# Expert stage of a decoder layer on one Trainium2 core: the rows of two tiles turned together at every second tile

## The chip, the core and the metric

The kernel runs on one core of a Trainium2 chip. Its engines run side by side, each with its own program, and wait for each other by semaphores: TensorE (PE in the profile; its weight loads are PEld), VectorE (DVE), ScalarE (ACT), GpSimd (POOL) and SyncE (SP), which here only issues DMAs. PE writes to PSUM; the other data lies in SBUF or, behind DMAs, in HBM. The metric is the device time of one execution in microseconds, as a median over runs.

## The reference

A decoder layer over 32 sequences of 256 tokens, 256 channels, in float32. Three blocks follow each other, each with a residual and a layer norm: a Mamba-2 mixer, cross attention to 77 context rows with 16 heads, and a mixture of experts. Only the last is touched by the change:

```python
scores = xt @ gate_w                                   # 8192 tokens, 8 experts
ew, ei = jax.lax.top_k(scores, K)                      # K = 2
ew = jax.nn.softmax(ew, axis=-1)
mask = ei[None, :, :] == jnp.arange(E)[:, None, None]
wE = jnp.sum(ew[None, :, :] * mask, axis=-1)
h = jax.nn.gelu(jnp.einsum('td,edf->etf', xt, w1) + b1[:, None, :], approximate=False)
o = jnp.einsum('etf,efd->etd', h, w2) + b2[:, None, :]
y = _layernorm(xt[None, :, :] + o, ln_g[:, None, :], ln_b[:, None, :])
out = jnp.einsum('et,etd->td', wE, y)
```

## The kernel before, in words

The stages are the mixer, keys and values, attention (which also sends every token's row to two places in HBM, sorted by expert), the experts, and a last stage that joins each token's two shares and normalises.

The expert stage (`experts_phase`) works on 71 tiles (2 x 8192 / 256 + 7) of 256 rows, each of one expert; a table in SBUF tells each tile's first row and expert. For tile t:

- SP loads the expert's first weights, `load_w1` (L1034, 1024 KB, high and low halves, into one of 4 places; and the bias, L1036), and then the tile's 256 rows, `load_rows` (L1041, 260 KB, into one of 8 buffers `xa`). It does so three tiles ahead: in step t it issues the weights of tile t + 3 and behind them the rows of tile t + 3. The weights' place is free once up and gelu of tile t - 1 are done, so SP waits for these (`s_h`, `s_gelu` of `t.ago(head.W)`). The first three tiles are loaded at the end of the attention stage.
- PE turns the rows, `turn_x` (L2010): four 128x128 transposes into one of two PSUM buffers `ps_x`. It waits for the tile's rows (`s_xa_in`) and for the low half of tile t - 2, which was read from the same PSUM buffer (`s_xlo`).
- ACT copies the turned rows as the high half `xT_hi` (`x_high`, L2054), DVE forms the low half `xT_lo` (`x_low`, L2090). Both wait until up of tile t - 2 is done, since that reads the same two-deep buffers.
- PE forms the hidden values, `up` (L112 to L114, into `ps_h`): 24 matmuls of 128x128 by 128x256, three for each product (high by high, high by low, low by high).
- ACT applies gelu (L2068) and takes the high half (`h_high`, L2077); DVE takes the low half (`h_low`, L2102).
- PE forms the output, `down` (L112 to L114, into `ps_o`), again 24 matmuls. The second weights of all experts stay in SBUF.
- DVE adds, takes the norm's statistics and scales; POOL adds the bias row, forms the inverse deviation, and sends the result back by an indirect DMA (L2197).

Each engine's order is written out by `run_steps`: a list of parts with lags, run for every tile; the first 8 tiles and the last ones are written out, the rest is a loop whose turn holds 8 tiles (`per=X`). `t.slot` is the tile's number modulo 8, `t.ago(-1)` the next tile. PE's list is: turn of the next tile, up of this tile, down of the tile before. Before the list starts, `turn_x` of tile 0 is run. The list is fixed; no planner or pool decides anything.

Of the kernel before, what the change touches and what calls it, by code (L numbers as in the profile page):

```python
# [77 lines left out]
def run_steps(eng, n, stages, spare=0, per=2, peel=PEEL):  # L78

    last = max(lag for _, lag in stages)
    turns = (n - spare - peel) // per
    after = peel + turns * per

    def peeled(s):
        for stage, lag in stages:
            if 0 <= s - lag < n:
                stage(Item(*divmod(s - lag, per), per))

    for s in range(peel):  # L90
        peeled(s)
    with eng.Fori(peel // per, peel // per + turns) as turn:
        for slot in range(per):
            for stage, lag in stages:
                stage(Item(turn, slot, per).ago(lag))
    for s in range(after, n + last):
        peeled(s)
# [10 lines left out]
def split3(eng, out, lhs, rhs, start, stop):  # L108

    (lh, ll), (rh, rl) = lhs, rhs
    eng.matmul(out, lh, rh, start=start, stop=False)  # L112
    eng.matmul(out, lh, rl, start=False, stop=False)  # L113
    return eng.matmul(out, ll, rh, start=False, stop=stop)  # L114
# [894 lines left out]
class ExpertsHead:  # L1009

    X = 8
# [900 lines left out]
def experts_phase(nc, signals, done_with, routing, b1, weights, w2, head):  # L1913
# [4 lines left out]
    n_tiles = routing.n_tiles  # L1918
    X = head.X

    with ExitStack() as ctx:
        def sb(name, shape, dt=F32):
            return ctx.enter_context(nc.sbuf_tensor("c_" + name, shape, dt))
# [7 lines left out]
        spare = sb("spare", [P, 1])  # L1931
# [40 lines left out]
        def expert_of(eng, t):  # L1972
            return eng.value_load(routing.table[0:1, 1, bass.ds(t.value(), 1)], min_val=0, max_val=E - 1)

        @block.sync
        def _(sp):
            def load_rows(t):
                if not t.before(X):
                    sp.wait_ge(s_xb, t.ago(X).count(1, 1))
                    sp.wait_ge(s_to, t.ago(X).count(1, 1))  # L1980
                    sp.wait_ge(s_share, t.ago(X).count(1, 1))
                    sp.wait_ge(s_x, t.ago(X).count(1, 1))
                    sp.wait_ge(s_os, t.ago(X).count(1, 1))
                head.load_rows(sp, routing, t)

            def load_w1(t):
                if not t.before(head.W):
                    sp.wait_ge(s_h, t.ago(head.W).count(1, 1))
                    sp.wait_ge(s_gelu, t.ago(head.W).count(1, 1))
                head.load_w1(sp, routing, b1, t)  # L1990

            def rows_ahead(t):
                if not (t.known() and t.value() + 3 >= n_tiles):
                    load_rows(t.ago(-3))

            def w1_ahead(t):
                if not (t.known() and t.value() + 3 >= n_tiles):
                    load_w1(t.ago(-3))

            run_steps(sp, n_tiles, [(w1_ahead, 0), (rows_ahead, 0)], spare=3, per=X, peel=8)  # L2000

        @block.tensor
        def _(pe):
            def turn_x(t):
                pe.wait_ge(s_xa_in[t.slot], t.turn * 16 + 16)
                if not t.before(2):
                    pe.wait_ge(s_xlo, t.ago(2).count(1, 1))
                for k in range(KD):
                    for c in range(NT):
                        last = pe.transpose(ps_x[t.par][:, T * k + P * c:T * k + P * c + P],  # L2010
                                            xa[t.slot][:, c, P * k:P * k + P], ident)
                last.then_inc(s_x, 1)

            def turn_x_next(t):
                if not (t.known() and t.value() + 1 >= n_tiles):
                    turn_x(t.ago(-1))

            def up(t):
                pe.wait_ge(s_w1_in[head.place(t)], head.loaded(t))
                pe.wait_ge(s_xhi, t.count(1, 1))  # L2020
                pe.wait_ge(s_xlo, t.count(1, 1))
                if not t.before(2):
                    pe.wait_ge(s_gelu, t.ago(2).count(1, 1))
                for m in range(MF):
                    for k in range(KD):
                        part, at = 2 * k + m // 2, slice(P * (m % 2), P * (m % 2) + P)
                        last = split3(pe, ps_h[t.par][:, m // 2, T * (m % 2):T * (m % 2) + T],
                                      (w1[head.place(t)][:, part, 0, at], w1[head.place(t)][:, part, 1, at]),
                                      (xT_hi[:, t.par, k, :], xT_lo[:, t.par, k, :]), k == 0, k == KD - 1)
                last.then_inc(s_h, 1)  # L2030

            def down(t):
                e = expert_of(pe, t)
                pe.wait_ge(s_hlo, t.count(1, 1))
                if not t.before(2):
                    pe.wait_ge(s_y, t.ago(2).count(NT, NT))
                for c in range(NT):
                    for m in range(MF):
                        at = slice(T * m + P * c, T * m + P * c + P)
                        last = split3(pe, ps_o[t.par][:, D * c:D * c + D], (h_hi[:, t.par, at], h_lo[:, t.par, at]),  # L2040
                                      [w2[:, bass.ds(MF * e + m, 1), h, :].rearrange("p o d -> p (o d)")
                                       for h in range(2)], m == 0, m == MF - 1)
                last.then_inc(s_o, 1)

            turn_x(Item(0, 0, X))
            run_steps(pe, n_tiles, [(turn_x_next, 0), (up, 0), (down, 1)], spare=3, per=X, peel=8)

        @block.scalar
        def _(act):
# [400 lines left out]
```

## Time and profile before

| | |
|---|---|
| median of 3 runs | 2335.59 us (2334.3 to 2337.23) |
| the profiled execution | 2338.11 us, its span 2336.3 us |
| PE busy over the span | 2146.5 us, 92% |
| DVE, ACT, POOL busy | 73%, 62%, 49% |
| mean granted clock of PE | 0.943 |
| the expert stage | about 1779 to 2229 us of the span |

Times in the profile count from the span's start. Shares over the whole span mix stages that have different limits, so the expert stage has to be looked at by itself.
### The profile page before, as it was taken

Reading aid. Unit: us, or ns where it says so; the run is one execution under the profiler, and the core shown is the slowest. Engines: PE = TensorE matmul, PEld = TensorE weight load, DVE = VectorE, ACT = ScalarE, POOL = GpSimd, SP = SyncE. Lnnn points to the kernel's source line nnn. Section 1 sums busy time; section 2 is a strip of 40 time slices with the busy share of each in tenths; the row PEclk is TensorE's granted clock in tenths of the full one; section 3 lists DMA queues with packets and bytes.
Section 4 is the critical chain, followed back from the end, with each engine's and each line's share of the span. In section 5 each row is a group of like instructions: output and inputs, shape, how many; then the busy total and the mean of one; then the engine's idle time right before and its main releaser. Section 6 shows DMA issues by size and latency. Waiting matters only on the chain. (4 is left out here: it accounts for less than half of the span.)

```text
span 2336.3 us, 53128 instructions
## 1 busy us (share of the span) xinstructions
PE 2146.5 (92%) x15740; PEld 1915.1 (82%) x15741; DVE 1717.0 (73%) x4450; ACT 1444.1 (62%) x3032; POOL 1153.9 (49%) x1376
## 2 busy tenths in 40 slices
PE   6989999898997797999999999999995999999968
PEld 5878888787886786888888888888885999999934
DVE  5877778787776324677776777767764999999956
ACT  6777777777775333666666666666662555555525
POOL 2556565555655001234343443334332777777767
PEclk8999999999998898999999999999997999999955
DMA  4443443434342353232222222222215878787658
GB/s 131 149 159 131 142 147 130 159 113 159 127 146 100 138 206 118 68 97 77 72 76 71 82 67 74 74 81 73 67 47 178 262 253 260 255 262 254 197 165 290
DMA packets 200152, 330.44 MB, mean 141 GB/s; under 512 B 26300, under 2 KB 87492, under 8 KB 200068
## 3 DMA queue, kind: packets, MB, share of 16 engines
q1 hardware_dynamic: 187108, 293.75, 38.5%
q0 software_dynamic: 12960, 35.67, 4.1%
q8 instruction: 41, 0.67, 0.1%
q14 instruction: 43, 0.35, 0.0%
HBM read 176.20 MB, written 153.15 MB: 141 GB/s over the span
## 5 line engine op out<-in xcount | busy, mean ns | idle before, releaser
L1605 ACT ACTIVATE b_wk_f<-b_ps_s,b_nmx 128x77 f32<-128x77 f32 x1024 | 233.7, 347 | 17.5 <-DVE b_nmx L1651 17.5
L619 DVE SCALAR_TENSOR_TENSOR a_conv<-a_xc_pad,a_cw,a_conv 128x256 f32<-128x256 f32 x384 | 218.7, 630 | 2.6 <-ACT a_conv L493 2.6
L1613 ACT ACTIVATE b_pT<-b_ps_pT 77x1024 f32<-77x1024 f32 x128 | 130.7, 1021 | 141.2 <-PE b_ps_pT L1511 141.2
L2068 ACT ACTIVATE c_hid<-c_ps_h,c_b_c 128x256 f32<-128x256 f32 x284 | 111.3, 475 | 159.8 <-PE c_ps_h L114 157.7
L2197 POOL DMA_INDIRECT made_scratch<-c_o_s,c_to x142 | 164.1, 1155 | 87.4 <-issue 49.9
L1876 POOL DMA_INDIRECT sent_scratch<-b_x_t,b_pos x128 | 128.4, 1003 | 141.8 <-DVE b_x_t L1747 102.0
L1667 DVE TENSOR_TENSOR k_wk_lo<-b_ps_oT,k_wk_lo 128x512 fp32r<-128x512 f32 x128 | 88.0, 688 | 128.3 <-ACT k_wk_lo L1619 100.6
L1596 ACT ACTIVATE b_qT<-b_ps_q,b_bq_s 128x256 f32<-128x256 f32 x256 | 107.5, 471 | 105.9 <-PE b_ps_q L114 104.7
L1892 POOL CAST w<-k_c_f 128x256 f32 (+1 forms) x32 | 14.7, 460 | 318.0 <-DMA k_c_f<-in_c_w 318.0
L112 PE MATMUL c_ps_o<-w,c_h_hi 128*128 x568 | 162.2, 286 | 6.9 <-DVE c_h_lo L2102 6.8
L114 PE MATMUL c_ps_o<-w,c_h_lo 128*128 x568 | 161.1, 284 | 0.0
L1499 PE MATMUL b_ps_s<-b_kz,b_qT 128*128 128x154 f32 x1024 | 156.3, 294 | 5.2 <-ACT b_wk_f L1605 5.1
L113 PE MATMUL c_ps_o<-w,c_h_hi 128*128 x568 | 161.0, 284 | 0.0
L112 PE MATMUL b_ps_out<-b_wo_hi,k_wk_lo 128*128 128x256 f32 x512 | 158.3, 309 | 0.0
L112 PE MATMUL b_ps_q<-k_wk_hi,b_wq_hi 128*128 128x256 f32 x512 | 154.3, 301 | 2.4 <-DVE k_wk_hi L1643 1.5
L1499 PEld LDWEIGHTS b_ps_s<-b_kz,b_qT 128*128 128x128 f32 x1024 | 140.4, 189 | 6.0 <-issue 6.0
L113 PE MATMUL b_ps_out<-b_wo_lo,k_wk_lo 128*128 128x256 f32 x512 | 144.5, 282 | 0.0
L114 PE MATMUL b_ps_q<-k_wk_hi,b_wq_lo 128*128 128x256 f32 x512 | 143.6, 281 | 0.0
L113 PE MATMUL b_ps_q<-k_wk_hi,b_wq_hi 128*128 128x256 f32 x512 | 143.6, 280 | 0.0
L114 PE MATMUL b_ps_out<-b_wo_hi,k_wk_lo 128*128 128x256 f32 x512 | 143.5, 280 | 0.0
L1524 PE MATMUL b_ps_oT<-b_pT,b_vv 77*64 77x256 f32 x1024 | 138.8, 392 | 0.0
L112 PEld LDWEIGHTS b_ps_out<-b_wo_hi,k_wk_lo 128*128 128x128 f32 x512 | 96.3, 188 | 48.9 <-issue 48.9
(314 smaller groups left out, 7776.6 us busy)
## 6 DMA issues: line engine op xcount, KB each, us to landing
sent_scratch<-r_none SPq DMA_DIRECT2D x90, 780.0 KB, 6.0
b_wq_hi<-parts_scratch SPq DMA_DIRECT2D x18, 1024.0 KB
b_wq_lo<-parts_scratch SPq DMA_DIRECT2D x18, 1024.0 KB
k_wk_hi<-parts_scratch SPq DMA_DIRECT2D x18, 1024.0 KB
k_wk_lo<-parts_scratch SPq DMA_DIRECT2D x17, 1024.0 KB
d_got<-made_scratch SPq DMA_DIRECT2D x32, 512.0 KB, 5.0
keys_scratch<-k_k_s SPq DMA_DIRECT2D x8, 1232.0 KB, 4.7
b_kz<-keys_scratch SPq DMA_DIRECT2D x64, 154.0 KB, 2.8
```

The lines of the kernel that those rows point to most:

```text
L112: eng.matmul(out, lh, rh, start=start, stop=False)
L113: eng.matmul(out, lh, rl, start=False, stop=False)
L114: return eng.matmul(out, ll, rh, start=False, stop=stop)
L619: dve.scalar_tensor_tensor(out=conv[:, m, :], in0=xc_pad[:, m, k:k + L], scalar=cw[:, m, k:k + 1], in1=conv[:, m, :], op0=ALU.mult, op1=AL ...
L1499: last = pe.matmul(s_scores[:, i, 2 * j:2 * j + 2, :], qT[:, u.par, i, P * j:P * j + P], kz[:, b.par, :, GM * g + i, :], start=True, stop= ...
L1524: last = pe.matmul(ps_oT[HD * a:HD * a + HD, L * i:L * i + L], vv[:, b.par, at:at + HD], pT[:, u.par, i, L * a:L * a + L], start=True, sto ...
L1596: last = act.activation(qT[:, u.par, i, :], ps_q[:, L * i:L * i + L], ACT.Identity, bias=bq_s[:, m:m + 1], scale=HD ** -0.5)
L1605: last = act.activation(pe_[:, u.par, c, :], s_scores[:, c // (C // GM), c % (C // GM), :], ACT.Exp, bias=nmx[:, u.par, c:c + 1])
L1613: act.activation(pT[:, u.par, :, :], ps_pT[0:LK, :, :], ACT.Copy).then_inc(s_pTc, 1)
L1876: pool.indirect_dma_start(routing.sent, bass.IndirectOffsetOnAxis(pos[:, b.par, 2 * c + n:2 * c + n + 1], 0), x2_t[:, b.par, c, :], None). ...
L2068: last = act.activation(hid[:, t.par, T * m:T * m + T], ps_h[t.par][:, m // 2, T * (m % 2):T * (m % 2) + T], ACT.Gelu, bias=b1_c[:, head.p ...
L2197: pool.indirect_dma_start(routing.made, bass.IndirectOffsetOnAxis(to[:, t.slot, c:c + 1], 0), o_s[:, t.par, c, :], None).then_inc(s_sent[t ...
```

## The change

PE's list gets another first part. It does nothing at odd tiles. At an even tile t it turns the rows of tile t + 1 and of tile t + 2, one behind the other. Up, down, all other engines' lists and all buffers are as before.

```diff
-            def turn_x_next(t):
-                if not (t.known() and t.value() + 1 >= n_tiles):
-                    turn_x(t.ago(-1))
+            def turn_next_two(t):
+                if t.slot % 2 == 0:
+                    for more in (1, 2):
+                        if not (t.known() and t.value() + more >= n_tiles):
+                            turn_x(t.ago(-more))
...
             turn_x(Item(0, 0, X))
-            run_steps(pe, n_tiles, [(turn_x_next, 0), (up, 0), (down, 1)], spare=3, per=X, peel=8)
+            run_steps(pe, n_tiles, [(turn_next_two, 0), (up, 0), (down, 1)], spare=3, per=X, peel=8)
```

The order of PE's instructions at the start of the stage, before. In brackets stand the semaphores that an instruction waits for, under the names of their first users: `a_na` is `s_xlo` here, `a_l` is `s_xhi`, `a_sp` is `s_gelu`; `c_xa_in1` tells of the rows in buffer 1, `c_w1_in0` of the weights in place 0. The tiles `b_wk_f`, `b_w_stage` and `k_c_f` hold the row buffers, `b_mk` the identity, `b_wq_*` and `k_wk_*` the weights.

```order
L2010 MATMUL c_ps_x<-b_mk,b_wk_f 128x128 [waits c_xa_in0]
L2010 MATMUL c_ps_x<-b_mk,b_wk_f 128x128 x3
L2010 MATMUL c_ps_x<-b_mk,b_wk_f 128x128 [waits c_xa_in1]
...
L112 MATMUL c_ps_h<-c_xT_hi,b_wq_hi 128x256 [waits a_na,a_l,c_w1_in0]
L113 MATMUL c_ps_h<-c_xT_lo,b_wq_hi 128x256
```

And after the change, at the same place on PE:

```order
L2010 MATMUL c_ps_x<-b_mk,b_wk_f 128x128 [waits c_xa_in0]
L2010 MATMUL c_ps_x<-b_mk,b_wk_f 128x128 x3
L2010 MATMUL c_ps_x<-b_mk,b_wk_f 128x128 [waits c_xa_in1]
...
L2010 MATMUL c_ps_x<-b_mk,b_wk_f 128x128 [waits a_na,c_xa_in2]
...
L112 MATMUL c_ps_h<-c_xT_hi,b_wq_hi 128x256 [waits a_na,a_l,c_w1_in0]
L113 MATMUL c_ps_h<-c_xT_lo,b_wq_hi 128x256
```

The turn of tile 2 now stands ahead of the first up, and so does its wait for the rows in buffer 2 (its three further transposes, and those of tile 1, are left out, since they read alike). The second place is the even tile 2 and the odd tile 3 on PE, as a piece of the difference:

```order
 L2010 MATMUL c_ps_x<-b_mk,b_w_stage 128x128 [waits a_na,c_xa_in3]
 L2010 MATMUL c_ps_x<-b_mk,b_w_stage 128x128 x3
+L2010 MATMUL c_ps_x<-b_mk,b_w_stage 128x128 [waits a_na,c_xa_in4]
+L2010 MATMUL c_ps_x<-b_mk,b_w_stage 128x128 x3
 L112 MATMUL c_ps_h<-c_xT_hi,k_wk_hi 128x256 [waits a_na,a_sp,a_l,c_w1_in2]
 L113 MATMUL c_ps_h<-c_xT_lo,k_wk_hi 128x256
...
 L114 MATMUL c_ps_o<-w,c_h_lo 128x256
-L2010 MATMUL c_ps_x<-b_mk,b_w_stage 128x128 [waits a_na,c_xa_in4]
-L2010 MATMUL c_ps_x<-b_mk,b_w_stage 128x128 x3
 L112 MATMUL c_ps_h<-c_xT_hi,k_wk_lo 128x256 [waits a_na,a_sp,a_l,c_w1_in3]
 L113 MATMUL c_ps_h<-c_xT_lo,k_wk_lo 128x256
```

The turn of tile 4, with its wait for the rows in buffer 4 and for `s_xlo` of tile 2, moved from in front of up(3) to in front of up(2). The same holds for every even tile up to 70.

## Rows read from the trace of the kernel before

**Rows 1.** The page: GB/s moved, in 40 slices of the span.
```profile
GB/s 131 149 159 131 142 147 130 159 113 159 127 146 100 138 206 118 68 97 77 72 76 71 82 67 74 74 81 73 67 47 178 262 253 260 255 262 254 197 165 290
```

**Rows 2.** Windows: busy us of PE, PEld, DVE, ACT, POOL; clock, DMA share, GB/s.
```profile
1900.00:2000.00 100.00, 100.00 (x854) 100.00 (x853) 97.18 (x298) 53.81 (x101) 78.43 (x82) 1.00 0.79 260
```

**Rows 3.** Timeline of PE: start us, us, engine, line, operation, out<-in, shapes.
```profile
1993.94 0.60 PE L2010 MATMUL c_ps_x<-b_mk,b_w_stage 128*128 128x128 f32 x4
1994.29 0.37 PE L112 MATMUL c_ps_h<-c_xT_hi,k_wk_hi 128*128 128x256 f32 x1
1994.50 0.28 PE L113 MATMUL c_ps_h<-c_xT_lo,k_wk_hi 128*128 128x256 f32 x1
1994.61 0.28 PE L114 MATMUL c_ps_h<-c_xT_hi,k_wk_hi 128*128 128x256 f32 x1
...
1997.11 0.28 PE L112 MATMUL c_ps_o<-w,c_h_hi 128*128 x1
...
2006.33 0.36 PE L112 MATMUL c_ps_h<-c_xT_hi,b_wq_hi 128*128 128x256 f32 x1
...
2012.13 0.60 PE L2010 MATMUL c_ps_x<-b_mk,k_c_f 128*128 128x128 f32 x4
```

**Rows 4.** Timeline of DVE, same step.
```profile
1995.20 1.21 DVE L2102 TENSOR_TENSOR c_h_lo<-c_hid,c_h_hi 128x1024 fp32r<-128x1024 f32 x1
```

**Rows 5.** Waits from 1820 to 2240: who <- whom: us in total, times, longest.
```profile
PE c_ps_o L112 <- DVE c_h_lo L2102: 4.6, 4, 2.8
```

**Rows 6.** Timeline of ACT, same step; in brackets the idle time before.
```profile
1997.36 1.57 ACT L2068 ACTIVATE c_hid<-c_ps_h,c_b_c 128x256 f32<-128x256 f32 x4 [2.19 <-PE c_ps_h L114]
```

**Rows 7.** DMAs that SyncE issues, timeline.
```profile
1776.74 0.37 SPq L1041 DMA_DIRECT2D b_wk_f<-sent_scratch  x1
...
1999.93 0.37 SPq L1034 DMA_DIRECT2D k_wk_hi<-parts_scratch  x1
...
2001.90 0.37 SPq L1041 DMA_DIRECT2D k_c_f<-sent_scratch  x1
```

**Rows 8.** Windows at the load of tile 38.
```profile
2000.00:2000.50 0.50, 0.50 (x6) 0.50 (x5) 0.50 (x3) 0.02 (x1) 0.42 (x1) 1.00 0.00 0
2005.50:2006.00 0.50, 0.50 (x7) 0.50 (x6) 0.50 (x2) 0.50 (x1) 0.45 (x1) 1.00 0.57 223
2006.00:2006.50 0.50, 0.50 (x7) 0.50 (x6) 0.50 (x2) 0.04 (x1) 0.44 (x1) 1.00 0.04 16
```

**Rows 9.** Timeline of DVE at the start of the stage.
```profile
1781.23 0.69 DVE L2090 TENSOR_TENSOR c_xT_lo<-c_ps_x,c_xT_hi 128x512 fp32r<-128x512 f32 x1 [1.67 <-ACT c_xT_hi L2054]
```

**Rows 10.** Timeline of PE at the start of the stage.
```profile
1779.48 1.94 PE L2010 MATMUL c_ps_x<-b_mk,b_wk_f 128*128 128x128 f32 x8 [17.41 <-PEq L1281]
1782.07 0.55 PE L112 MATMUL c_ps_h<-c_xT_hi,b_wq_hi 128*128 128x256 f32 x1 [0.65 <-ACT c_xT_hi L2054]
...
1792.85 0.38 PE L112 MATMUL c_ps_o<-w,c_h_hi 128*128 x1 [2.17 <-DVE c_h_lo L2102]
```

**Rows 11.** Windows beside up(4), up(32), up(50) and up(68).
```profile
1809.72:1810.22 0.50, 0.50 (x7) 0.50 (x6) 0.50 (x6) 0.22 (x1) 0.42 (x2) 1.00 0.05 12
...
1981.52:1982.02 0.50, 0.50 (x7) 0.50 (x6) 0.50 (x2) 0.20 (x1) 0.50 (x1) 1.00 1.08 404
...
2091.47:2091.97 0.50, 0.50 (x7) 0.50 (x6) 0.50 (x2) 0.21 (x1) 0.38 (x2) 1.00 0.67 261
...
2202.95:2203.45 0.50, 0.50 (x7) 0.50 (x6) 0.47 (x2) 0.00 (x0) 0.50 (x1) 1.00 0.40 139
```

**Rows 12.** Windows at the start of the stage.
```profile
1770.50:1781.00 10.50, 1.52 (x7) 1.55 (x8) 0.06 (x1) 0.40 (x1) 0.00 (x0) 0.50 0.80 251
1782.00:1786.00 4.00, 3.93 (x18) 3.96 (x19) 0.69 (x1) 0.06 (x1) 0.00 (x0) 0.50 1.05 390
1794.00:1797.00 3.00, 3.00 (x16) 3.00 (x15) 1.23 (x1) 0.46 (x1) 0.00 (x0) 0.50 1.07 386
```

**Rows 13.** DMA issues: out<-in, count, KB each, median us to landing.
```profile
b_xa<-x_scratch SPq DMA_DIRECT2D x32, 256.0 KB, 2.7
```

## Prediction

> **What bounds the kernel now.** I read the page first, then the busy sums by stretch, then each engine's timeline within one step of the expert stage, and last the share of the DMA engines in windows of half a microsecond. The page's slices show the DMA rate tripled in the last quarter: that is the expert stage [rows 1]. Between 1900 and 2000 us the tensor engine (PE) is busy 100% at a granted clock of 1.00, VectorE (DVE) 97%, ScalarE (ACT) 54%, GpSimd (POOL) 78%, the DMA engines 79% [rows 2]. So PE sets the pace there and DVE is close behind. What makes PE wait in this stage goes into the time; what only frees another engine doesn't.
>
> T(k) is the turn of tile k (four transposes), up(k) and down(k) its two products. PE's timeline has T(35) at 1993.94, up(34) from 1994.29, down(33) from 1997.11, and T(38) at 2012.13: three steps in 18.19 us, 6.06 each, with no gap [rows 3]. DVE's low half of the hidden values of tile 33 is ready at 1996.41 (1995.20 + 1.21), 0.70 before down(33) starts [rows 3, 4]. From 1820 to 2240 PE waits 4 times for DVE, 4.6 us together, 2.8 of them in one; the rest, 1.8, is what DVE costs PE [rows 5].
>
> **The change, part by part.** The numbers of transposes, matmuls, loads and activations stay. T(odd) stays at its place, ahead of up of the even tile before it. T(even) moves forward over one up and one down, and over the waits that these have.
>
> (a) Entries. From the turn's first transpose to the second matmul of up it is 0.56 us (1993.94 to 1994.50), five starts at 0.112; a plain matmul comes 0.11 after its predecessor (1994.50, 1994.61) [rows 3]. The mixture costs at most 0.01 us per entry, 34 entries fewer give 0.4. Bounds: 0; and, if the first matmul's 0.37 us against 0.28 [rows 3] were lost time, 34 x 0.09 = 3.1. I take 0.4, since starts tell the pace and ends are modelled.
>
> (b) Shift inside a pair. Up(even) and down(odd) come one turn later, 0.35 us (1993.94 to 1994.29 [rows 3]); the next up and down stand at their old time. ACT waits 2.19 us for up [rows 6], so it starts the gelu of even tiles 0.35 later and still meets the 0.70 of DVE's lead, which itself grows by 0.35 for odd tiles. Nothing.
>
> (c) The new wait. Here I expect the time to go. T(k) needs the 256 rows of tile k. Take k = 38. SyncE issues its loads when gelu(34) is done: the weights at 1999.93, the rows behind them at 2001.90 [rows 7]. The DMA share is 0.00 in 2000.0 to 2000.5, still 0.57 in 2005.5 to 2006.0, and 0.04 after that [rows 8]. The rows are last in the queue, so they are there at about 2005.9. T(38) is at 2012.13 today, 6.2 us later. In the changed program it stands right behind T(37), at 2006.33, where up(36) begins today [rows 3]. Up(34), and with it gelu(34) and the load, is 0.35 later by (b), so the rows come at about 2006.25; from a release to PE's first matmul it takes 0.15 more (x_low ends at 1781.92, up(0) starts at 1782.07 [rows 9, 10]). 2006.4 against 2006.33: a lead of a whole step has become nothing. When T(k) waits, up(k-2), down(k-3) and all of PE's queue stand behind it; later loads hang on later gelus, so they move too and the loss is not made up.
>
> How often, and how much? For each even k from 6 to 70 (33 tiles) I took the half microsecond before the start of up(k-2) and the one after it. The earlier window begins where, in today's clock, the rows would have to be there (start - 0.35 - 0.15). In 9 of the 33 the second window still has a share of 0.05 or more: late by 0.5 to 1.0, I take 0.75, sum 6.75. In 19 only the first has: late by 0 to 0.5, I take 0.25, sum 4.75. In 5 neither has. [Rows 11] are the second window of tile 6 (first tile), the first windows of 34 and 52, and the first of 70 (last tile). A share of 0.06 is one of 16 DMA engines, and one is enough to hold a load up. Sum 11.5. Bounds: some of the nine (6, 18, 54, 66) show more in the second window than in the first and may be other transfers; with the other 5 at 0.5 alone it is 2.5; with 9 at 1.0 and 19 at 0.5 it is 18.5.
>
> The Trainium skill ("DMA: Bandwidth & Descriptors", section "Why a DMA increments its semaphore by 16 and not by 1") says that only the full 16 increments mean that all data is there, because the engines finish independently. It speaks against this change. The small shares at the end of the loads agree with it; by a rule that a load is as good as landed when most engines are done, the sum above would be near its lower bound, 2.5.
>
> (d) Start of the stage. Today T(0) and T(1) start at 1779.48, up(0) at 1782.07, and T(2) is done before PE's idle 2.17 us that end with down(0) at 1792.85 [rows 10]; there it costs nothing. Changed, T(2) stands ahead of up(0) and needs rows issued at 1776.74 [rows 7]. Asked for until then: two tiles' weights and three tiles' rows, 2 x 1.05 + 3 x 0.27 = 2.9 MB. Moved: 10.5 us x 251 KB = 2.64 MB up to 1781.0, the rest at 390 KB per us: done at 1781.7; with the next weights, which share the engines, at 1784.4 [rows 12]. I take 1783.0. On the half clock (0.50, 18 matmuls in 3.93 us [rows 12]) four transposes take 0.87, so up(0) starts at about 1784.0, 1.9 late. If the clock rises when it does today, the matmuls put off run at full speed and 1.1 is left; if it rises as long after up(0), 1.9. I take 1.4. Bounds: 0.5 (rows there at once) and 4.7 (rows at 1784.4, and 1.5 more on half clock after a longer idle).
>
> (e) What goes. With PE slower, DVE catches up, and PE's 1.8 us for DVE mostly go: -1.5 (bounds 0 and -1.8).
>
> Sum: -0.4 + 11.5 + 1.4 - 1.5 = +11.0 us. The profiled execution took 2338.11, its span 2336.3; it becomes 2349.1. The median of the runs shown, 2335.59, lies 2.5 below it; with the same difference the median becomes 2346.6. What a measurement of this kernel can't tell from no change is 0.2%, 4.7 us.
>
> **Rivals.**
> No change: the loads land in time. DMAs, less crowded by the wider gap before even tiles, end a few tenths earlier. For it: many of the 19 first windows have a share of only 0.07 to 0.2. Against it: 1.08 and 0.67 at tiles 34 and 52 [rows 11]. Term (c) at its lower bound: -0.4 + 2.5 + 1.4 - 1.5 = +2.0, 2337.6. Chance 0.16.
>
> Faster: entries cost what the durations say. -3.1 - 1.8 = -4.9, with all loads in time and a start that costs nothing: 2330.7. It wins only if (c) is below about 3 us. Chance 0.05.
>
> Slower still, by the clock. After the idle 2.17 us before 1792.85 the clock stands at 0.50 in 1794 to 1797, where 16 matmuls take 3.0 us [rows 10, 12]; at the 0.115 of [rows 3] they would take 1.8. If waits of a microsecond or two bring this about five times, 6 us, and (c) is 18.5: -0.4 + 18.5 + 1.4 - 1.5 + 6 = +24.0, 2359.6. For it: an idle PE is what preceded that fall. Against it: most of the waits are under half a microsecond. Chance 0.13.
>
> Slower by the landing. A load of 256 KB in another stage takes 2.7 us to landing [rows 13], of which 0.7 is moving at 390 KB per us and 0.6 or more goes before the first byte (1999.93 to after 2000.5); up to 1.4 may pass between the last byte and the semaphore. If the windows leave that out, each of the 33 tiles is 1.4 later, 46 us: 2393. Against it: the shares count the engines until they report. Chance 0.03. The skill's page has the same thing in "Anatomy of one DMA — SWDGE (gpsimd) path", as a fixed part of some 2 us, most of it waiting for the write's receipt; no row here separates it.
>
> **Numbers.** Forecast 0.61, its own range 2341 to 2354; the rivals 0.16, 0.05, 0.13, 0.03; that the order of instructions isn't as shown, 0.02, no change. Slower by over 0.2% (above 2340.3) is 0.61 + 0.13 + 0.03 + 0.01 = 0.78; within 0.17; faster 0.05. The range of all, 2337 to 2357, takes in the rival of no change and most of the way to the clock's.
>
> **What would show it.** Right: waits of PE (or its weight loads) in the turn, ended by the load of rows, at 20 to 28 even tiles, most under 1 us, the longest at few tiles; a pair of steps of 12.1 us growing to about 12.4; DVE busy near 95%; fewer waits of PE for DVE; up(0) at about 1784. Wrong: PE without gaps from 1900 to 2000 and a span within 3 us: then the rows land earlier than the shares say. Wrong in the other direction: a granted clock below 1.00 inside the stage.

## The result and the profile after

| | before | after |
|---|---|---|
| median, us | 2334.95 (2333.21 to 2337.23) | 2359.3 (2353.13 to 2369.24) |
| the profiled execution, us | 2338.11 | 2360.27 |
| its span; mean granted clock | 2336.3; 0.943 | 2358.5; 0.945 |
| up(0), up(70) start at | 1782.07, 2215.37 | 1779.75, 2236.89 |

The ratio is 1.0107, with a 95% interval of 1.0087 to 1.0126: slower by 24.4 us, where 11 had been forecast, and outside the range. Here and below, medians of the kernels with an edit leave out slow executions, those over 1.5% above the fastest of the same kernel; for the kernel before this would make 0.03 us of difference at most.

Of the 22.2 us between the spans 21.5 are there when up(70) starts. They are made up of three parts. From up(3) to up(70) it is 411.7 us before and 436.3 after, 24.6 more. From T(0) to up(3) it is 24.2 and 25.5, 1.3 more. And T(0) itself, with which the stage begins on PE, came 4.4 us sooner in the changed kernel's execution (1775.07, against 1779.48 in [rows 10]), which can't come from the change, since T(0) stands ahead of it on PE; other executions of the kernels below have T(0) anywhere from 1767 to 1780. So the loss is made in the expert stage, nearly all of it behind its start. Lines of the code are two higher after the change (L2102 is now L2104); L2010 is unchanged.

The page after, its row of GB/s in 40 slices, answers to [rows 1]: 262, 253, 260, 255 have become 245, 236, 242, 240. The stage moves the same bytes in more time.

```profile
GB/s 139 141 156 158 117 158 129 141 157 117 158 117 104 152 216 101 72 83 74 83 69 73 72 80 72 71 75 75 71 42 238 245 236 242 240 241 242 197 163 289
```

Windows of the changed kernel (us; busy of PE, PEld, DVE, ACT, POOL; clock; DMA share; GB/s), the first against [rows 2]:

```profile
1900.00:2000.00 100.00, 94.42 (x793) 92.83 (x792) 94.70 (x271) 47.49 (x90) 69.52 (x76) 1.00 0.73 236
...
1793.20:2247.00 453.80, 429.96 (x3599) 422.21 (x3598) 431.49 (x1242) 218.16 (x413) 315.02 (x341) 1.00 0.72 231
```

PE is no longer busy all the time, 94.4 us of 100 with 793 matmuls instead of 854. Every other engine is less busy too. VectorE, at 94.7, stands level with PE, but it was at 97.2 before; what bounds the stage has to be read from what PE waits for. The granted clock is 1.00 from 1793.2 to 2247. Who PE waits for is in the waits from 1795 to 2260 (who <- whom: us in total, times, longest), against [rows 5]:

```profile
PEld c_ps_x L2010 <- issue: 23.5, 26, 1.7
PE c_ps_x L2010 <- DMA b_wk_f<-sent_scratch: 8.8, 12, 1.4
PE c_ps_x L2010 <- DMA k_c_f<-sent_scratch: 6.1, 7, 1.5
...
PE c_ps_o L112 <- DVE c_h_lo L2104: 5.0, 4, 2.8
PE c_ps_x L2010 <- DMA b_w_stage<-sent_scratch: 3.7, 6, 1.0
```

The new waits are the three on `sent_scratch`, the rows, in the turn: 25 times. (The 23.5 us of PEld stand before the same turns: its weight loads stand still with PE.) Measured from start to start of PE's instructions (0.12 apart where nothing waits), it is 30 places of the 34 pairs, 23.3 us, median 0.72, longest 1.63; before there is none. Each of them lies between the two turns of a pair. Late downs, counted in the same way at the first two matmuls of each down, are 3.4 us at 12 places before and 2.1 at 5 after.

### The profile page after: what moved, and what is told of

Its sections match the earlier page's. It is cut to its first block and busy times, and to the rows that moved or that the text cites. A ratio compares the mean times of both kernels' runs of the same rounds, so it can differ in the third digit from the quotient of the medians.

```text
span 2358.5 us, 53121 instructions
## 1 busy us (share of the span) xinstructions
PE 2148.0 (91%) x15740; PEld 1909.4 (81%) x15741; DVE 1731.0 (73%) x4450; ACT 1440.1 (61%) x3032; POOL 1147.4 (49%) x1376
```

## One circle, and why it has a length

The timeline of the changed kernel from up(32) to up(34) (start us, us, engine, line, operation, out<-in, and idle time before with what ended it). SPq rows are SyncE's issues.

```profile
1991.14 0.65 PE L2010 MATMUL c_ps_x<-b_mk,b_wk_f 128*128 128x128 f32 x4 [1.15 <-DMA b_wk_f<-sent_scratch]
1991.55 0.36 PE L112 MATMUL c_ps_h<-c_xT_hi,b_wq_hi 128*128 128x256 f32 x1
...
1993.80 0.96 POOL L2199 DMA_INDIRECT made_scratch<-c_o_s,c_to  x1 [0.30 <-issue]
...
1994.36 0.28 PE L114 MATMUL c_ps_h<-c_xT_hi,b_wq_hi 128*128 128x256 f32 x1
...
1995.48 1.57 ACT L2070 ACTIVATE c_hid<-c_ps_h,c_b_c 128x256 f32<-128x256 f32 x4 [4.77 <-PE c_ps_h L114]
...
1997.93 0.37 SPq L1034 DMA_DIRECT2D b_wq_hi<-parts_scratch  x1
...
2000.08 0.19 SPq L1041 DMA_DIRECT2D b_w_stage<-sent_scratch  x1
...
2004.64 0.65 PE L2010 MATMUL c_ps_x<-b_mk,b_w_stage 128*128 128x128 f32 x4 [1.01 <-DMA b_w_stage<-sent_scratch]
2005.04 0.36 PE L112 MATMUL c_ps_h<-c_xT_hi,k_wk_hi 128*128 128x256 f32 x1
```

Read it as a circle: T(34) waited for its rows, so up(32) is at 1991.55; gelu(32) ends at 1997.05 and lets SyncE issue the weights of tile 36 at 1997.93 and its rows at 2000.08; they are all there at 2004.52; T(36) starts 0.12 us later, and up(34) at 2005.04. That is 13.49 us for a pair of steps, in which PE has work for 12.25. The pieces, as means over the even tiles 8 to 66 of each trace, all in us (up to gelu's end; to the weights' issue; to the rows' issue; to their landing; to the next even up):

| profile | pieces | pair | late increments | late rows issues |
|---|---|---|---|---|
| before | 4.79, 0.97, 1.98, 4.36, (no wait) | 12.29 | 6 | 2 |
| changed, first time | 5.00, 0.90, 2.19, 4.45, 0.57 | 13.10 | 23 | 6 |
| changed, fourth time | 4.74, 0.90, 1.95, 4.55, 0.55 | 12.69 | 0 | 0 |

The fourth time is the run of the last comparison below. The first line shows what could have been worked out ahead of the change: its four pieces add up to 12.10 us, and with the 0.57 from the landing to the next even up the circle would be 12.67. That is 0.38 over the pair of 12.29, times 33 pairs 12.5 us, an estimate.

Two things are counted at the right. A late increment is one of the semaphore behind up (`s_h`): by the trace's semaphore events it comes 0.29 us after the start of up's last matmul, but at 23 of 71 tiles of the first trace 0.47 to 1.08 us after, at nearly all of them 1.3 to 1.6 us behind the start of one of POOL's indirect sends. Above, the last matmul starts at 1994.36 and gelu 1.12 us later; at most tiles it is 0.37. A late rows issue is one where SyncE needs 3.0 us and not 1.95 from the weights to the rows, as here for tile 40, with POOL's two sends beside it (timeline of the changed kernel):

```profile
2024.32 0.37 SPq L1034 DMA_DIRECT2D b_wq_hi<-parts_scratch  x1
2024.49 1.04 POOL L2199 DMA_INDIRECT made_scratch<-c_o_s,c_to  x1 [0.71 <-issue]
...
2025.83 0.96 POOL L2199 DMA_INDIRECT made_scratch<-c_o_s,c_to  x1 [0.30 <-issue]
...
2027.26 0.01 SPq L1041 DMA_DIRECT2D b_wk_f<-sent_scratch  x1
```

## Experiments

Each diff is against the changed kernel, where nothing else is said. "Before" is the kernel before, run in the same comparison.

**Is it the wait for rows?** SyncE issues the rows ahead of the weights, some 5 us sooner; once with pairs, once in the kernel before.

```diff
-            run_steps(sp, n_tiles, [(w1_ahead, 0), (rows_ahead, 0)], spare=3, per=X, peel=8)
+            run_steps(sp, n_tiles, [(rows_ahead, 0), (w1_ahead, 0)], spare=3, per=X, peel=8)
```

> The changed kernel, but SyncE issues in each step the rows of tile t+3 before the weights of tile t+3, so the rows no longer stand behind the wait for gelu of tile t-1 nor behind a megabyte of weights. Theory A (the time goes into T(even) waiting for its rows): the waits of PE in L2010 for a load disappear, PE has no gaps in the stage, and the time is that of the kernel before, 2333 to 2338 us. Rival B (two turns in a row, or up and down of a pair shifted by a turn, cost by themselves, by the hidden values coming later to ACT and DVE): the time stays above 2350 us. Rival C (half of each): about 2345.

> The kernel before with the same swap of SyncE's two loads: the control for the experiment above. The rows are early anyway, so theory A says no change: 2335 us within 0.2%. If the order of loads were worth something by itself (weights later, fewer collisions), it would show here and would have to be taken off the run above; a loss would show as PE waiting for the weights in up.

Pairs: 2340.36 against 2333.18, ratio 1.0032 [1.0008, 1.0056]. Single turns: 2333.01, 1.0006 [0.9986, 1.0026]. No wait was left in the turn, so the rows were the cause of those. But with pairs another loss stood in their place: late downs of 17.7 us at 31 places (1.7 with single turns). After the longest of them, an idle PE for 2.06 us before a down at 2119.71, the granted clock was 0.50 from 2120.5 to 2123.5, where 16 matmuls took 3.0 us. Waits from 1795 to 2260, that window, and one of VectorE's smallest operations beside POOL's bias addition:

```profile
PE c_ps_o L112 <- DVE c_h_lo L2104: 16.6, 13, 2.7
```

```profile
2120.50:2123.50 3.00, 3.00 (x16) 3.00 (x16) 2.92 (x10) 0.00 (x0) 2.22 (x3) 0.50 0.63 198
```

```profile
2099.79 1.84 DVE L2143 TENSOR_SCALAR c_ve<-c_mv 128x2 f32<-128x2 f32 x1
2100.28 1.31 POOL L2176 TENSOR_TENSOR c_xb<-b_wk_f,b_w_stage 128x512 f32<-128x512 f32 x1
2102.81 1.21 DVE L2104 TENSOR_TENSOR c_h_lo<-c_hid,c_h_hi 128x1024 fp32r<-128x1024 f32 x1
2104.30 0.38 PE L112 MATMUL c_ps_o<-w,c_h_hi 128*128 x1 [1.52 <-DVE c_h_lo L2104]
```

VectorE's 128x2 operation ends with POOL's addition (2101.63 and 2101.59), 1.84 us where it takes 0.17 alone; 11 of 71 took over 1.5 us here, 3 before. The Trainium skill ("SBUF — State Buffer", section "SBUF: two separate sides") says that the two engines share a pair of ports, and that whichever of their operations starts first holds it for its whole instruction while the other stands. That the two end together agrees with one being held by the other. That the one recorded as starting first (2099.79 against 2100.28) is the one held does not agree, as far as POOL's recorded start is exact, and the measurement decides. Of VectorE the section names only operations in a two-port mode or with two inputs in SBUF; whether this one is of that kind no row shows.

**The size of the circle.** The rows go between the weights and the bias, instead of behind both.

```diff
-        sp.dma_start(self.b1_c[:, self.place(t), :], b1[bass.ds(e, 1), :, :].rearrange("o p m -> (o p) m")
-                     ).then_inc(self.s_w1_in[self.place(t)], 16)
+        return lambda: sp.dma_start(self.b1_c[:, self.place(t), :], b1[bass.ds(e, 1), :, :].rearrange("o p m -> (o p) m")
+                                    ).then_inc(self.s_w1_in[self.place(t)], 16)
...
+                    load_bias = load_w1(t.ago(-3))
+                    load_rows(t.ago(-3))
+                    load_bias()
```

> The changed kernel, but SyncE issues the 2 KB of bias behind the rows and not between weights and rows. The rows are issued about 0.56 us earlier; everything else stays. Theory A with a cycle that closes over two steps (turn, up, gelu, load, turn of the next even tile): every even tile that waits gets about 0.5 us less, so 34 x 0.5 = 17 us of the 24 go, and the time is 2340 to 2348. Theory A without the cycle (each wait a separate accident of a late DMA, as I forecast): those accidents stay and it is above 2350. Rival B (pairs cost by themselves): no difference, 2355 to 2362.

2340.33, ratio 1.0034 [1.0021, 1.0047]. The rows' issue came 1.38 us behind the weights and not 1.95, but from there to their landing it took 4.96 instead of 4.55 (the changed kernel's fourth profile, taken on another chip, but like this one without late increments). Of 0.56 us 0.41 were lost again; that the weights ahead in the queue still have to move would explain it, but is not shown by itself. What is left made the pair 12.50 instead of 12.69, times 33 is 6 us; the waits are 6.8 us at 27 turns, median 0.18, instead of 11.7, and the time 7 us less against before (+7.2, +14.1). The time follows the circle; the expected 17 us took the landing as fixed.

**The same pairs with a longer lead.** The second turn stands behind up instead of ahead of it.

```diff
-            run_steps(pe, n_tiles, [(turn_next_two, 0), (up, 0), (down, 1)], spare=3, per=X, peel=8)
+            run_steps(pe, n_tiles, [(turn_more(1), 0), (up, 0), (turn_more(2), 0), (down, 1)], spare=3, per=X, peel=8)
```

`turn_more(n)` turns tile t + n at even t.

> The changed kernel with T(t+2) of the even tile moved behind up(t), ahead of down(t-1): 3 us later than in the change, 3 us earlier than in the kernel before. Up and down of a pair shift as little as before. Theory A: a lead of some 3 us over the landing is enough, no wait, 2333 to 2338 us. Rival D (an early turn costs by itself because its PSUM buffer, ACT's x_high or DVE's x_low come in another order): half of the loss or more stays, above 2345.

2330.62, ratio 0.9991 [0.996, 1.0021]; no wait in the turns, late downs 3.6 us, up(3) to up(70) 410.9. Three microseconds later, the rows are always there, in a comparison whose profiles had no late increments.

**The start of the stage, and the rest without it.** Once only the turn of tile 2 moves; once the pairs begin at tile 2.

```diff
-                if t.slot % 2 == 0:
-                    for more in (1, 2):
-                        if not (t.known() and t.value() + more >= n_tiles):
-                            turn_x(t.ago(-more))
+                first = t.known() and t.value() == 0
+                if not (t.known() and t.value() in (1, n_tiles - 1)):
+                    for more in (1, 2) if first else (1,):
+                        turn_x(t.ago(-more))
```

```diff
-                if t.slot % 2 == 0:
-                    for more in (1, 2):
+                single = t.known() and t.value() < 2
+                if single or t.slot % 2 == 0:
+                    for more in (1,) if single else (1, 2):
```

> Only the turn of tile 2 moves ahead of up(0); from there on each turn stands one tile ahead, as before the change. Theory of the cycle (all of the loss is made anew at each even tile, the start costs nothing): 2333 to 2335 us, ratio 1.000 to 1.001, up(3) to up(70) 411 to 413 us. Rival, the prediction's term for the start: +1.4 us, and by its upper bound +4.7. A rival beyond both: a late start puts all engines of the stage into another phase, in which the loads stay late; then up(3) to up(70) is well above 413 here as well.

> The complement: the first turns stand as before the change, pairs begin at the even tile 2. Theory of the cycle: the whole loss, 2356 to 2360 us, ratio about 1.010, 28 to 33 waits in the second turn of a pair with 21 to 25 us. Rival, the start carries part of it: 2350 or less.

Start alone: 2334.32 against 2333.12, 1.0004 [0.9985, 1.0024]. Pairs from tile 2 on: 2345.51, 1.0054 [1.0025, 1.0083], with 11.2 us of waits at 25 turns. The two parts add up to 13.6 us, where the whole change had lost 24.4. This profile had no late increment.

**VectorE and POOL.** POOL adds the bias row behind the inverse deviation, with pairs and rows first, and in the kernel before.

```diff
-            run_steps(pool, n_tiles, [(add_b2, 1), (scale, 2), (send_back, 3)], spare=3, per=X, peel=8)
+            run_steps(pool, n_tiles, [(scale, 2), (add_b2, 1), (send_back, 3)], spare=3, per=X, peel=8)
```

> Pairs, with the rows issued ahead of the weights, and besides POOL adds the bias row after the inverse deviation and no longer before it. In the kernel with rows first alone there were no waits for rows, but 19 us of waits of PE for VectorE's low half; in the stretches with these waits VectorE's smallest operation (c_ve, 128x2) took up to 1.8 us beside POOL's bias addition, instead of 0.17. Theory D (this collision is what makes VectorE late): c_ve goes to 0.2 to 0.5 us everywhere, PE's waits for VectorE drop under 5 us, time 2333 to 2336. Rival E (VectorE is late because gelu of even tiles starts 0.35 us later behind the pair, and only its lead counts): waits of 10 us or more remain although c_ve is short, 2340 us or more. Rival F: the addition collides with VectorE's other operations at its new place, and VectorE's whole step gets longer.

> The kernel before the change with POOL's bias addition behind the inverse deviation, as a control for the run with pairs. Theory D: within 0.2% of before, perhaps 1 to 3 us faster, since PE's 3.4 us of late downs go. Rival F: slower by 3 us or more, by a longer step of VectorE.

2398.19 and 2396.25, ratios 1.0278 [1.0251, 1.0305] and 1.0274 [1.0246, 1.0302]. Rival F has the sign, and theory D is left undecided, because the edit changed more than the collision. The short operation did fall, from a mean of 588 ns in the kernel before to 203, but VectorE now waits for POOL's sends (28.7 us in 200 over its three groups of `c_o_s`). DVE groups of the second kernel from 1900 to 2100 (busy, mean ns, idle before and what ended it):

```profile
L2156 DVE SCALAR_TENSOR_TENSOR c_o_s<-c_tt,c_rw,b_wk_f 128x256 f32<-128x256 f32 x24 | 12.2, 550 | 11.6 <-DMA made_scratch<-c_o_s,c_to 11.5
...
L2141 DVE TENSOR_SCALAR c_ve<-c_mv 128x2 f32<-128x2 f32 x28 | 5.7, 203 | 1.0
```

**Is the changed kernel's 24 us repeatable?** The two kernels again, the rows-first one again, and both cures together.

> The changed kernel itself once more, beside the kernel before, on another day or chip than the first comparison. In its first profile an even tile's circle (rows there, up, gelu, weights issued, rows issued, rows there) measured 5.00 + 0.90 + 2.19 + 4.45 + 0.57 = 13.1 us, in the run with pairs from tile 2 on 4.73 + 0.90 + 1.94 + 4.55 + 0.54 = 12.65. The first difference, 0.27, are increments of the semaphore behind up that came 0.5 to 0.8 us late at 20 of 71 tiles, the second, 0.25, rows issues of SyncE that came 3.0 instead of 1.95 us behind the weights at 6 even tiles. Theory G: both are a disturbance of that run and not of the program; the changed kernel then measures 2344 to 2349 here, ratio 1.005 to 1.007, and the profile shows pairs of steps of about 12.65 us. Rival H: the early turn of tile 2 at the start is what puts the stage into that phase; then this run gives 2353 to 2362 again, ratio about 1.010, with late increments at 15 tiles or more.

> The kernel before the change itself, for its profile. In its first profile 5 tiles had a late increment behind up (0.54 to 1.26 us after the last matmul's start instead of 0.29). Theory G: none or one here, up(3) to up(70) 410 to 413 us. Rival H: 3 to 7 of them again.

> Pairs with the rows issued ahead of the weights, once more, since its times spread from 2332 to 2353. Theory: the load waits are gone for good (none at the turns), and what is left is PE waiting for VectorE's low half, 5 to 25 us depending on the run; median 2338 to 2350, ratio 1.001 to 1.007. Rival: it was a disturbance, then within 0.1% of before and waits for VectorE under 5 us.

> The second turn of a pair stands behind up instead of ahead of it, and the rows are issued between the weights and the bias. Both give the rows more lead: some 3 us by the place and 0.56 by the issue. Theory of the cycle: 12.2 us of PE work per pair against a circle of about 9.5 us, so no wait at the turns, and the time is that of before, ratio 0.998 to 1.001. That a pair also saves switches between turn and product is worth at most 1 us. Rival: VectorE's low halves come late as in the kernel with rows first, ratio above 1.002.

Changed: 2357.62 against 2334.1, 1.0104 [1.0086, 1.0122], 25.0 us of waits at 29 turns, 23 late increments, pairs of 13.06; theory G fell as it was put. Before: 2339.49 in its one run, 413.8 from up(3) to up(70), 3 late increments. Rows first: 2334.72, 1.001 [0.9994, 1.0027], single executions from 2333.48 to 2342.11; its profile, of one that took 2339.92, has 14.1 us of late downs and again a fall of the granted clock to 0.50, after an idle PE for 2.90 us. Both cures: 2336.98, 1.0015 [0.9995, 1.0034], no wait at the turns although 5 increments were late, late downs 4.3 us, 411.5 from up(3) to up(70). It is no better than the second turn behind up alone.

**Start, chip, or POOL's sends?** The last has POOL send ahead of the inverse deviation:

```diff
-            run_steps(pool, n_tiles, [(add_b2, 1), (scale, 2), (send_back, 3)], spare=3, per=X, peel=8)
+            run_steps(pool, n_tiles, [(add_b2, 1), (send_back, 3), (scale, 2)], spare=3, per=X, peel=8)
```

> The changed kernel a third time, beside the kernel with pairs from tile 2 on, in one comparison. Both kernels with about +24 us were profiled with 20 or more late increments of the semaphore behind up; the kernel with pairs from tile 2 on had none and +12, and so had nothing of the kind in any kernel measured in the same comparison. Theory J (the lateness goes with the chip or the occasion): both kernels have the same time here, within 4 us, either both about 2345 without late increments or both about 2357 with them. Rival H (the early turn of tile 2 sets the phase): this one 2353 or more, the other 2349 or less.

> As the run before it: theory J, the same time as the changed kernel within 4 us, and late increments in both or in neither. Rival H: 2349 or less with no late increments, beside a changed kernel of 2353 or more with them.

> Pairs with the rows issued 0.56 us earlier. Theory of the cycle: 0.56 us per pair less to wait, 33 x 0.56 = 18 us, as long as there is that much to wait. If the changed kernel loses 24 us here, this one loses 6 to 9 (2340 to 2343); if it loses 12, this one 2 to 5 (it can't fall below PE's own 12.2 us per pair). First time: 2340.3, +7.

> The changed kernel, with POOL sending a tile's result ahead of the inverse deviation and not behind it, so that its second send no longer starts 0.6 to 0.8 us before the end of up and no longer beside SyncE's issue. Theory K (the sends hold up the increments and the rows issue of the even tiles): fewer than 5 late increments, no rows issue 3.0 us behind the weights, a pair of steps 12.65 us, 2345 to 2349. Rival L: the waits stay as many and as long as in the changed kernel. Rival M: POOL's changed order makes VectorE late, as did the bias addition behind the inverse deviation (2396), and the time is above 2365.

Before 2334.82. Changed 2355.67, 1.0074 [1.0045, 1.0103]; pairs from tile 2 on 2360.77, 1.0094 [1.0068, 1.012]; the intervals overlap, and the medians are 5 apart, where theory J had asked for 4 at most. The profiles have 22 and 24 late increments, pairs of 13.05 and 13.23. So the early turn of tile 2 is not what brings the larger loss, and the same program that had lost 12 us lost 26 here. Rows between weights and bias: 2347.42, 1.0042 [1.0015, 1.0069], above the expected 2340 to 2343, with 12 late increments, a pair of 12.77 and 14.8 us of waits; from the issue to the landing 4.91 against 4.47, so here again most of the 0.56 was lost. A pair 0.28 shorter, times 33, is 9 us, and 8 were measured. Sends first: 2369.4, 1.0129 [1.0062, 1.0196]. The waits for rows fell to 8 us at 20 turns, though 19 of 30 rows issues were late (2.71 on the mean) and 12 increments. In their place stood late downs of 31.7 us, and behind them VectorE, which waited for POOL's weighting (waits from 1820 to 2240):

```profile
DVE c_o_s L2158 <- POOL c_rw L2189: 47.4, 63, 2.6
...
PE c_ps_o L112 <- DVE c_h_lo L2104: 21.5, 27, 1.9
```

So theory K's cure fell, and rival M has the sign. Like the moved bias addition, this edit changed more than what it was meant to single out.

**The changed kernel where the increments are in time.**

> The changed kernel a fourth time. Theory J: its time goes with the late increments. With fewer than 5 of them in its profile 2344 to 2349 and a circle of 12.6 to 12.7 us, with 15 or more 2353 to 2361 and 13.0 to 13.2. Rival: 2353 or more with fewer than 5, or 2349 or less with 15 or more; then something else sets the size.

> Pairs with the second turn behind up, again. Its circle has some 3 us to spare, so late increments of 0.5 to 0.8 us can't reach TensorE: 2330 to 2336, within 0.2% of before whether or not there are late increments. Rival: with late increments it is above before by 0.2% or more.

Before 2332.88. Changed: 2346.98, ratio 1.0058 [1.0041, 1.0076], no late increment, none of the rows issues late, 11.7 us of waits at 29 turns. The step from up(32) to up(34) of this profile, against the one above:

```profile
1979.35 0.65 PE L2010 MATMUL c_ps_x<-b_mk,b_wk_f 128*128 128x128 f32 x4 [0.21 <-DMA b_wk_f<-sent_scratch]
...
1981.86 1.01 POOL L2199 DMA_INDIRECT made_scratch<-c_o_s,c_to  x1 [0.30 <-issue]
...
1982.57 0.28 PE L114 MATMUL c_ps_h<-c_xT_hi,b_wq_hi 128*128 128x256 f32 x1
...
1983.02 1.57 ACT L2070 ACTIVATE c_hid<-c_ps_h,c_b_c 128x256 f32<-128x256 f32 x4 [3.16 <-PE c_ps_h L114]
...
1985.47 0.37 SPq L1034 DMA_DIRECT2D b_wq_hi<-parts_scratch  x1
...
1987.45 0.37 SPq L1041 DMA_DIRECT2D b_w_stage<-sent_scratch  x1
...
1992.23 0.65 PE L2010 MATMUL c_ps_x<-b_mk,b_w_stage 128*128 128x128 f32 x4 [0.40 <-DMA b_w_stage<-sent_scratch]
1992.63 0.36 PE L112 MATMUL c_ps_h<-c_xT_hi,k_wk_hi 128*128 128x256 f32 x1
```

The send starts 0.71 us before up's last matmul, as it did above (0.56), but gelu follows after 0.45 and not 1.12; the wait is 0.40 and not 1.01. The form with the second turn behind up: 2332.65, 1.0002 [0.9986, 1.0017], again without late increments, so how it stands up to them was not seen. Nothing tried beats the kernel before.

## Why the prediction was wrong

Its sign and its mechanism held, its size did not: 24.4 us were lost, more than twice the 11.0 of the sum. By its steps:

(c) The new wait, +11.5, is the step that failed: 23.3 measured, beyond its upper bound of 18.5. The mechanism was right, and the term was mis-sized. It took the load's times from the trace of before and moved them by 0.35 only ("Up(34), and with it gelu(34) and the load, is 0.35 later"). But the pieces of the circle are not those of before: with POOL's sends at another place of the step, increments behind up came late at 23 tiles (+0.26 on the mean from up to gelu's end, against the fourth run's profile) and six rows issues a microsecond late (+0.24), while the landing took 0.10 less. These 0.41 us for each pair, times 33, are 13.5 us that the sum did not have.

In the fourth run of the changed kernel, where neither happened, the waits were 11.7 us at 29 places, and its median, 2346.98, would have lain in the forecast's range. The reading of the loads was right for that case: by the semaphore events of the trace of before, which are incomplete at a few tiles, and with the prediction's own shift of 0.35, the rows would come late at 22 tiles for about 12 us together (an estimate). The spread over the tiles was wrong all the same. The prediction saw that later loads hang on later gelus, but not that they close a circle of fixed length, which makes nearly every pair late: 30 waits of 0.7 in the first run, not 9 of 0.75 and 19 of 0.25 with 5 tiles in time. That the totals of 11.5 and 11.7 come so close is partly luck.

How much hangs on it: the changed kernel lost 24.4, 23.5 and 20.9 us in the three comparisons with 22 or more late increments, 14.1 in the one without; pairs from tile 2 on 25.9 with, 12.4 without. Pairs of 13.05 to 13.23 against 12.65 to 12.69, times 33, is 12 to 19 us. The kernel before has 6 and 3 late increments in its two traces, and its medians stay within some 2 us over all comparisons, which fits the whole step of lead that its rows have.

(d) The start, +1.4, was right. PE at the start of the stage, after the change:

```profile
1775.07 1.94 PE L2010 MATMUL c_ps_x<-b_mk,b_wk_f 128*128 128x128 f32 x8 [17.66 <-PEq L1281]
1778.98 1.12 PE L2010 MATMUL c_ps_x<-b_mk,b_wk_f 128*128 128x128 f32 x4 [1.97 <-DMA b_wk_f<-sent_scratch]
1779.75 0.56 PE L112 MATMUL c_ps_h<-c_xT_hi,b_wq_hi 128*128 128x256 f32 x1
```

T(2) waited 1.97 us for its rows. In span time that is 1778.98 and not 1783.0, but the whole stage had begun 4.4 us sooner. From T(0) to up(0) it is 4.68 us after the change and 2.59 before, 2.1 more where 1.9 had been expected, and at up(3) 1.3 of it are left. Alone, the early T(2) measured +1.2 us, which can't be told from nothing by the time, though the profile shows the wait.

(e) Late downs, -1.5: 3.4 became 2.1, -1.3, as expected.

(a) Entries, -0.4: the undisturbed pairs are 12.25 us in both; under 1 us for the stage, not resolved.

(b) "Nothing" is right only while PE waits for rows. With these waits taken away, late downs of 17.7 and 14.1 us appeared in the two profiles with rows first. That gelu of even tiles is 0.35 later and DVE's lead of 0.70 with it shorter is in line with that; that the collision with POOL's addition then feeds the delay is argued, since both attempts to move it changed POOL's step more than it.

The rivals: "no change" needed rows in time. The clock's 2359.6 came nearest in microseconds and was wrong in kind: with waits of up to 1.63 us the clock stayed at 1.00. Inside the stage it fell once in each of the two profiles with rows first, after PE had stood 2.06 and 2.90 us for VectorE. The landing, 1.4 us for each tile, did not show: the turn starts 0.12 to 0.18 us after the last increment, and in the trace of before the last increment of tile 38's rows is at 2005.94, where the shares had put their end at 2005.9. The section that the prediction names for this rival is, in the Trainium skill, on the path of DMAs that GpSimd issues; these loads are SyncE's. Of the signs that were named, the waits came (at 30 tiles, not 20 to 28), VectorE stood at 95% and waits for it became fewer; the pair grew to 13.10 us and not to 12.4.

Open: why the increments are late in some comparisons and not in others. In the first pair of traces and in two comparisons every profile had some of them (3 to 24), in the other three comparisons no profile of any kernel had one; each comparison ran on one chip, so chip and occasion can't be told apart. In the changed kernel nearly all come 1.3 to 1.6 us after the start of a send of POOL, yet in the profiles without any late increment sends stand at the same place and delay nothing.

## What to carry to other kernels

When a wait moves ahead of the work that releases the buffer for the next load, write down the circle: wait, compute, release, issue, landing. If it is longer than the engine's own work in that time, every turn pays the difference, and a tenth of a microsecond in any piece is multiplied by the number of turns. Durations from the trace before are then only a first guess, since the new cadence puts other work beside each piece. With half a step of lead (here 3 us) no wait was left in any of three profiles; of these one had late increments (5), and it had the bias moved as well.

## What was not expected of the hardware

- An increment of a semaphore by PE came up to 0.8 us late in the changed kernel, mostly beside an indirect DMA of POOL: 0.29 us after the matmul's start normally, 0.47 to 1.08 at the late tiles (0.54 to 1.26 at six tiles of the kernel before), in some comparisons only.
- SyncE's third issue came 3.0 us behind its first instead of 1.95 when POOL's indirect sends began beside it, at 6 even tiles of the changed kernel and at 19 of 30 when POOL sent sooner.
- Moving POOL's 1.3 us addition behind its 0.9 us power operation cost 63 us of 2333 in the kernel before, and 65 with pairs and rows first: the sends came later, and VectorE waited for them.
- VectorE's 128x2 operation took 0.17 us alone and up to 1.88 beside POOL's 128x512 addition.
